# Expert results added to the output: the order of two waits, a third result buffer, and weights converted in halves

## The chip, the cores and the metric

The kernel runs on one core of a Trainium2 chip. The metric is the device time of one execution in microseconds (us), the median over the timed runs. Beside it there is one execution with the hardware profiler, whose time and trace are used for every duration below. In it PE is TensorE's matmul row, DVE is VectorE, ACT is ScalarE, POOL is GpSimd and SP is SyncE.

## The reference

The input `x` has 8 x 256 = 2048 tokens of 256 numbers. A gated cross-attention picks two of 64 sets for each token and adds their weighted mean; then a gated mixture of experts follows, in which each token goes to 2 of 8 experts. The second part takes most of the time:

```python
x = x + jnp.tanh(g_xattn[0]) * _L0_xattn_ref(_layernorm(x), ctx_2048, ...)
x = x + jnp.tanh(g_ffn[0]) * _L0_ffn_ref(_layernorm(x), ...)
# in _L0_ffn_ref, for each of 8 experts (256 -> 1024 -> 256), w the token's weight for it:
h = jax.nn.gelu(xf @ w1 + b1, approximate=False)
y = h @ w2 + b2
acc = acc + y * w[:, None]
```

## The kernel before

**First stage** (to about 80 us). Tokens are loaded, attention and routing are computed, and `x` after attention is written to `out` in device memory. The normalised rows go to `xrows`. A table is made that sorts the 4096 pairs of token and expert by expert into 36 tiles of 128 rows. 32 tiles belong to one expert each; four, tiles 25, 28, 31 and 34 (`mixed_of`, `MIXED_AT`, `MIXED_STEP`), hold 64 rows of one expert and 64 of another.

**Weights.** There are 16 units (`NU`), fc1 and fc2 of each expert, each 128 x 2048 in fp32 in its own region of `wreg`. A unit is converted into two fp16 parts, the high part by ACT (`weights_hi`, L934) and the remainder by DVE (`weights_lo`, L1566), which waits for ACT by the semaphore `w_hi` and reports by `w_lo`. The parts go to the region that the unit ahead has left, so ACT's next unit waits for `w_lo`. Units 0 and 1 are done ahead of tile 0 in halves of 1024 columns (`first_hi`, `first_lo`, L925 and L1559). `units_of_tile` (L394) names the tile in whose place each other unit stands: unit 2 at tile 1, 3 at 3, then 4 to 15 at tiles 4, 6, 8, 10, 12, 14, 16, 17, 19, 20, 22, 23. `unit_ready` is PE's wait for a unit.

**A tile** i passes through these steps, each in the order of its engine's own program; semaphores alone tie the engines together.

- POOL fetches its 128 rows by an indirect DMA (`fetch_rows`, L1843), five tiles ahead; SP transposes them by a DMA.
- PE multiplies by the fc1 weights in 8 chunks of 128 columns, 6 matmuls each (L704). Between these chunks stand the chunks of fc2 for earlier tiles, 3 matmuls each (L730): the second half of tile i-2, then the first half of tile i-1. A mixed tile's fc2 comes all at once after the next tile's fc1.
- ACT applies GELU in two halves (L1018); DVE splits each half into two fp16 parts (`split`, L1736 and L1738), for which fc2 waits.
- DVE scales fc2's result and adds the bias (`add_bias`, L1695) into one of two buffers `y_sb`; ACT multiplies by the token's weight (`weigh`, L1057) in place and reports by `y_ready`.
- POOL adds the 128 rows to `out` by an indirect DMA with accumulation (`add_tile`, L1864; a mixed tile's halves in two transfers, L1856 and L1860). A token appears in two tiles, so each transfer waits by the semaphore `added` until the one ahead has landed. `add_bias` waits for the add two tiles back, whose buffer it fills.

For a mixed tile DVE copies the second expert's weights into buffers of their own ahead of time: `keep_w1` (four copies, L1715) two tiles ahead, `keep_w2` (L1727) one tile ahead; fc1 of the mixed tile waits for the first. `keep_w1` of tile 25 also waits until all units are converted.

A wait written right ahead of an instruction isn't always an instruction of its own. Of several waits in a row the built program puts one into the instruction itself, the last of the list in the rows of order below; the others become wait instructions ahead of it.

Of the kernel before, what the change touches and what calls it, by code (L numbers as in the profile page):

```python
# [5 lines left out]
ALU = mybir.AluOpType  # L6
ACT = mybir.ActivationFunctionType
AX = mybir.AxisListType
# [25 lines left out]
def flamingo_block(nc, x, ctx_sets, token_sets, g_xattn, g_ffn, desc, w_q, b_q, gate_w, gate_b,  # L34
# [42 lines left out]
    with ExitStack() as stack:  # L77
# [162 lines left out]
        by_half = table_buf[:, 2 * TILES * E:2 * TILES * E + 3 * E * E].rearrange("p (k s e) -> p k s e", k=3, e=E)  # L240
        half = sb("half", [P, 3, E])
        is_odd = sb("is_odd", [P, 2, MIXED], F16)
# [19 lines left out]
        def at_mixed(row):  # L262
# [129 lines left out]
        NARROW, WIDE = 160, 36  # L392
        units_of_tile = {1: (2,), 3: (3,)}
# [75 lines left out]
        def _(pe):  # L469
# [185 lines left out]
            def unit_ready(k):  # L655

                if k < 2:
                    pe.wait_ge(half_lo, 2 * k + 2)
                else:
                    pe.wait_ge(w_lo, k - 1)  # L660

# [21 lines left out]
            def fc1(i, c, ws):  # L683

                part_f = c // (FC // 2)
                if c == 0:
                    if i < FIRST_BY_PE:
                        pe.wait_ge(x0_sb, i + 1)
                    else:
                        pe.wait_ge(xT_in[i % NX], transposed(i))  # L690
                    if i == 0 or unit_for(i) != unit_for(i - 1):
                        unit_ready(unit_for(i))
                if c % (FC // 2) == 0 and i >= 2:
                    pe.wait_ge(gelu_done, 2 * (i - 2) + part_f + 1)
                if c == 0 and i in mixed_of:
                    pe.wait_ge(w1_kept, mixed_of[i] + 1)
                rows_each = P // len(ws)
                for h, of_half in enumerate(ws):
                    at = c % (FC // 2) * P + h * rows_each
                    put = bank[2 * (i % 2) + part_f][:, at:at + rows_each]  # L700
                    for k in range(KC):
                        hi, lo = of_half[k]
                        for n, (w, x_part) in enumerate(((hi, 0), (hi, 1), (lo, 0))):
                            mm = pe.matmul(put, w, xT[:, i % NX, x_part, k, h * rows_each:(h + 1) * rows_each],  # L704
                                           start=(k == 0 and n == 0), stop=(k == KC - 1 and n == 2))
                if c % (FC // 2) == FC // 2 - 1:
                    mm.then_inc(fc1_ps, 1)
# [111 lines left out]
        def _(act):  # L819
# [108 lines left out]

            def weights_hi(k, at):
                if k == 2:  # L930
                    act.wait_ge(half_lo, 4)
                else:
                    act.wait_ge(w_lo, k - 2)
                act.activation(whalf[:, bass.ds(at[1], 1), 0:UNIT].rearrange("p a n -> p (a n)"),  # L934
                               wreg[:, bass.ds(at[0], 1), :].rearrange("p a n -> p (a n)"),
                               ACT.Copy, scale=W_SCALE).then_inc(w_hi, 1)

            copy_pair(0, 0)
# [116 lines left out]
            def weigh(i):  # L1055
                act.wait_ge(y_biased, i + 1)
                act.activation(y_sb[:, i % 2, :], y_sb[:, i % 2, :], ACT.Copy,  # L1057
                               scale=wcur[:, i % NX:i % NX + 1]).then_inc(y_ready, 1)

            for i in range(TILES):  # L1060
                if i == TILES - 1:
                    weigh(i - 2)
                gelu(i, 0)
                if i == 0:
                    copy_rows(1)
                if 2 <= i < TILES - 1:
                    weigh(i - 2)
                if i + 1 < TILES:
                    fetch(i + 1)
                gelu(i, 1)  # L1070
                for k in units_of_tile.get(i, ()):
                    weights_hi(k, unit_regions(k))
            for i in range(TILES - 2, TILES):
# [3 lines left out]
        def _(v):  # L1077
# [381 lines left out]
            def odd_halves(k):  # L1459
# [35 lines left out]
                if k == 9:  # L1495
                    v.tensor_reduce(half[:, :, :], by_half, AX.X, ALU.add).then_inc(vec_step, 1)
                    done.up()
                if k == 10:
                    v.scalar_tensor_tensor(out=is_pair[:, :], in0=at_mixed(per_tile[:, 1, :]), scalar=0.0, in1=at_mixed(is_col),
                                           op0=ALU.is_gt, op1=ALU.mult).then_inc(halves_ready, 1)  # L1500
                    v.tensor_scalar(is_odd[:, :, :], half[:, 1, :].rearrange("p (m h) -> p h m", h=2), -1.0, iota_p[:, 0:1],
                                    ALU.add, ALU.is_equal).then_inc(halves_ready, 1)
                    v.tensor_tensor(code_m[:, :].rearrange("a (m h) -> a m h", h=2),
                                    half[0:1, 2, :].rearrange("a (m h) -> a m h", h=2),
                                    at_mixed(per_tile[0:1, 2, :]).unsqueeze(2).to_broadcast([1, MIXED, 2]),
                                    ALU.add).then_inc(vec_step, 1)
                    v.tensor_scalar(real_m[:, :, :], half[0:H, 0, :].rearrange("p (m h) -> p h m", h=2), iota_p[0:H, 0:1], None,
                                    ALU.is_gt).then_inc(vec_step, 1)
# [54 lines left out]

            def weights_lo(k, at):
                v.wait_ge(w_hi, k - 1)
                v.scalar_tensor_tensor(out=whalf[:, bass.ds(at[1], 1), UNIT:2 * UNIT].rearrange("p a n -> p (a n)"),  # L1566
                                       in0=wreg[:, bass.ds(at[0], 1), :].rearrange("p a n -> p (a n)"), scalar=W_SCALE,
                                       in1=whalf[:, bass.ds(at[1], 1), 0:UNIT].rearrange("p a n -> p (a n)"),
                                       op0=ALU.mult, op1=ALU.subtract).then_inc(w_lo, 1)

            pick_sets(0)
# [114 lines left out]
            def add_bias(i):  # L1686
# [3 lines left out]
                if i == 0:  # L1690
                    v.wait_ge(b2_in, 16)
                if i >= 2:
                    v.wait_ge(added, added_by(i - 2))
                for at, e in experts[i]:
                    op = v.scalar_tensor_tensor(out=y_sb[at, i % 2, :], in0=bank[ypos[i % 2]][at, 0:D],  # L1695
                                                scalar=1.0 / (H_SCALE * W_SCALE),
                                                in1=b2_all[at, bass.ds(e, 1), :].rearrange("p a d -> p (a d)"),
                                                op0=ALU.mult, op1=ALU.add)
# [4 lines left out]
            def keep_w1(m):  # L1703
                if m == 0:
                    v.wait_ge(w_lo, NU - 2)
                    v.wait_ge(out_init, 16 * NG)
# [12 lines left out]
            def keep_w2(m):  # L1719
                if m == 0:  # L1720
                    v.wait_ge(w_lo, NU - 2)
                if m >= 1:
# [21 lines left out]
            for i in range(TILES):  # L1744
# [8 lines left out]

                for k in units_of_tile.get(i - 1, ()):
                    if k < 4:
                        weights_lo(k, unit_regions(k))
                split(i, 1)
# [6 lines left out]
                if i == 18:  # L1764
                    odd_halves(13)
                for k in units_of_tile.get(i, ()):
                    if k >= 4:
                        weights_lo(k, unit_regions(k))
                if i + 2 in mixed_of:
# [7 lines left out]
        def _(pool):  # L1777
# [69 lines left out]
            def add_tile(i):  # L1847
                pool.wait_ge(y_ready, i + 1)
                if i >= 1:
                    pool.wait_ge(added, added_by(i - 1))  # L1850
                if i in mixed_of:

                    if i == MIXED_AT:
# [3 lines left out]
                        out=out[:, :], out_offset=bass.IndirectOffsetOnAxis(ap=add_m[:, 0, m:m + 1], axis=0),  # L1857
                        in_=y_sb[0:H, i % 2, :], in_offset=None, compute_op=ALU.add).then_inc(added, 16)
                    pool.wait_ge(added, added_by(i) - 16)
                    pool.indirect_dma_start(  # L1860
                        out=out[:, :], out_offset=bass.IndirectOffsetOnAxis(ap=add_m[:, 1, m:m + 1], axis=0),
                        in_=y_sb[H:P, i % 2, :], in_offset=None, compute_op=ALU.add).then_inc(added, 16)
                    return
                pool.indirect_dma_start(  # L1864
                    out=out[:, :], out_offset=bass.IndirectOffsetOnAxis(ap=add_at[:, i:i + 1], axis=0),
                    in_=y_sb[:, i % 2, :], in_offset=None, compute_op=ALU.add).then_inc(added, 16)

# [40 lines left out]
```

## Time and profile before

| | |
|---|---|
| median of the runs | 307.14 us (306.23, 307.14, 511.84) |
| profiled execution | 307.81 us |
| its span in the trace | 306.0 us |
| PE busy | 249.3 us (81% of the span) |
| DVE, ACT, POOL busy | 214.6, 182.9, 145.0 us |

The span is the time from the first to the last recorded event; the profiled execution's time is 1.8 us longer than its span, and 0.67 above the median. Busy shares are averages over stages with different limits, so the stages are read one by one. An idle time in a row belongs to the instruction behind it: "[0.84 <-DVE rows L1738]" says that the engine stood 0.84 us ahead of this instruction, and that DVE's instruction of line 1738 ended it.

### The profile page before, as it was taken

Reading aid. Unit: us, or ns where it says so; the run is one execution under the profiler, and the core shown is the slowest. Engines: PE = TensorE matmul, PEld = TensorE weight load, DVE = VectorE, ACT = ScalarE, POOL = GpSimd, SP = SyncE. Lnnn points to the kernel's source line nnn. Section 1 sums busy time; section 2 is a strip of 40 time slices with the busy share of each in tenths; the row PEclk is TensorE's granted clock in tenths of the full one; section 3 lists DMA queues with packets and bytes.
Section 4 is the critical chain, followed back from the end, with each engine's and each line's share of the span. In section 5 each row is a group of like instructions: output and inputs, shape, how many; then the busy total and the mean of one; then the engine's idle time right before and its main releaser. Section 6 shows DMA issues by size and latency. Waiting matters only on the chain.

```text
span 306.0 us, 9678 instructions
## 1 busy us (share of the span) xinstructions
PE 249.3 (81%) x3353; PEld 232.6 (76%) x3353; DVE 214.6 (70%) x679; ACT 182.9 (60%) x579; POOL 145.0 (47%) x122
## 2 busy tenths in 40 slices
PE   1999919734799999999999999998699999997100
PEld 1999818634699989999999999987698999996100
DVE  3898799997988778677777777767767666763100
ACT  1143869696684776866686776686474856573100
POOL 2121128994524657577454454366353635523330
PEclk9996955855899999999999999999799999999855
DMA  6999999986314434564635435346344342432220
GB/s 179 341 372 376 380 372 378 375 305 208 93 39 88 71 54 71 84 86 64 106 64 78 82 62 90 55 59 99 45 69 75 50 88 36 73 44 28 22 21 10
DMA packets 44575, 39.75 MB, mean 130 GB/s; under 512 B 21361, under 2 KB 41202, under 8 KB 44402
## 3 DMA queue, kind: packets, MB, share of 16 engines
q1 hardware_dynamic: 36912, 29.22, 31.3%
q0 software_dynamic: 6976, 9.59, 21.3%
q8 instruction: 29, 0.48, 0.7%
q10 hardware_dynamic: 642, 0.33, 0.4%
q14 instruction: 16, 0.13, 0.1%
HBM read 25.70 MB, written 8.98 MB: 113 GB/s over the span
## 4 chain that ended last, share of the span: by engine, by line
PE 40%; DMA 16%; DVE 14%; issue 9%; ACT 4%; POOL 2%; DVEq 1%; POOLq 0%; ACTq 0%
PE bank L704 21%; PE bank L730 18%; DMA out_dram<-xn,add_at 9%; DMA out_dram<-xn,add_m 6%; ACT wreg L934 2%; DVE wreg L1566 2%; ACT rows L1018 1%; DVE wreg L1237 1%; DVE rows L1228 1%; DVE xs L1207 1%; DMA xs<-xrows,fetch_at 1%; POOL out_dram L1856 1%; DVE earlier L1281 1%; DVE gmark L1271 1%; POOL out_dram L1864 1%
## 5 line engine op out<-in xcount | busy, mean ns | idle before, releaser
L730 PE MATMUL bank<-wreg,rows 128*128 (+1 forms) x864 | 135.8, 274 | 3.1 <-DVE rows L1738 3.1
L704 PE MATMUL bank<-xTp,wreg 128*128 128x128 f16 (+1 forms) x1728 | 132.5, 217 | 5.7 <-DVE pick_buf L1715 3.4
L704 PEld LDWEIGHTS bank<-xTp,wreg 128*128 x1728 | 113.1, 98 | 14.4 <-issue 7.0
L1018 ACT ACTIVATE rows<-bank,maskbias 128x128 f32<-128x128 f32 (+1 forms) x320 | 86.4, 363 | 24.2 <-issue 19.7
L1864 POOL DMA_INDIRECT out_dram<-xn,add_at x32 | 55.2, 1724 | 69.7 <-ACT maskbias L1049 34.3
L730 PEld LDWEIGHTS bank<-wreg,rows 128*128 128x128 f16 (+1 forms) x864 | 74.3, 99 | 7.3 <-issue 3.6
L1736 DVE TENSOR_SCALAR rows<-rows 128x512 f16<-128x512 f32 x72 | 31.9, 443 | 36.5 <-ACT rows L1018 36.2
L1738 DVE SCALAR_TENSOR_TENSOR rows<-rows 128x512 f16<-128x512 f32 x72 | 49.9, 693 | 2.5
L1843 POOL DMA_INDIRECT xs<-xrows,fetch_at x32 | 40.4, 1262 | 20.8 <-issue 9.1
L1057 ACT ACTIVATE xn<-xn,maskbias 128x256 f32<-128x256 f32 x36 | 18.5, 514 | 44.9 <-DVE xn L1695 44.9
L1566 DVE SCALAR_TENSOR_TENSOR wreg<-wreg x14 | 32.1, 2292 | 10.6 <-ACT wreg L934 9.7
L934 ACT ACTIVATE wreg<-wreg x14 | 26.9, 1919 | 2.1 <-DVE wreg L1566 1.9
L1804 POOL TENSOR_TENSOR rs<-ve,neg_half 128x4 f32<-128x4 f32 x8 | 8.4, 1050 | 34.6 <-DVE ve L1089 20.6
L1695 DVE SCALAR_TENSOR_TENSOR xn<-bank,xs 128x256 f32<-128x256 f32 (+1 forms) x40 | 16.8, 420 | 8.6 <-DMA out_dram<-xn,add_at 4.0
L830 ACT ACTIVATE xTp<-bank 128x512 f32<-128x512 f32 x8 | 4.8, 597 | 13.9 <-PE bank L477 13.9
L1856 POOL DMA_INDIRECT out_dram<-xn,add_m x4 | 6.1, 1534 | 13.9 <-DMA out_dram<-xn,add_at 7.4
L477 PE MATMUL bank<-ident,xs 128*128 128x128 f32 x32 | 7.2, 383 | 6.3 <-DMA xs<-in_x_dram 6.3
L1812 POOL TENSOR_SCALAR at_col<-iota,place_f,token 128x128 f16<-128x128 f32 x12 | 12.0, 1008 | 0.0
L490 PE MATMUL bank<-rhs_c,xTp 128*128 128x73 f32 x64 | 11.4, 336 | 0.0
L730 PE MATMUL bank<-xn,rows 128*64 128x256 f16 x80 | 11.2, 274 | 0.0
L490 PEld LDWEIGHTS bank<-rhs_c,xTp 128*128 128x128 f32 x64 | 10.7, 253 | 0.1
L477 PEld LDWEIGHTS bank<-ident,xs 128*128 128x128 f32 x32 | 6.0, 213 | 6.3 <-issue 6.3
(270 smaller groups left out, 338.2 us busy)
## 6 DMA issues: line engine op xcount, KB each, us to landing
wreg<-in_L_ffn_fc_w_dram SPq DMA_DIRECT2D x16, 1024.0 KB, 13.0
xrows<-rows SPq DMA_DIRECT2D x4, 528.0 KB, 5.9
xs<-in_x_dram SPq DMA_DIRECT2D x4, 512.0 KB, 8.8
out_dram<-xs SPq DMA_DIRECT2D x4, 512.0 KB, 8.6
xs<-in_L_ffn_fc_b_dram SPq DMA_DIRECT2D x1, 1024.0 KB, 5.9
xTp<-xs SPq DMA_TRANSPOSE x34
ctx_sb<-in_ctx_dram SPq DMA_DIRECT2D x1, 512.0 KB, 8.8
xs<-xrows,fetch_at POOLq DMA_INDIRECT x32
```

The source lines that it names most:

```text
L490: mm = pe.matmul(bank[2 + g % 2][:, q * NR:(q + 1) * NR], xTp[:, j, t, k, :], rhs_c[:, k, :], start=(k == 0), stop=(k == KC - 1))
L704: mm = pe.matmul(put, w, xT[:, i % NX, x_part, k, h * rows_each:(h + 1) * rows_each], start=(k == 0 and n == 0), stop=(k == KC - 1 and n = ...
L730: mm = pe.matmul(yb[at, :], h_part[:, at], of_half[w_part], start=(c == 0 and n == 0), stop=(c == FC - 1 and n == 2))
L934: act.activation(whalf[:, bass.ds(at[1], 1), 0:UNIT].rearrange("p a n -> p (a n)"), wreg[:, bass.ds(at[0], 1), :].rearrange("p a n -> p (a ...
L1018: op = act.activation(h32[i % 2][:, f * P:(f + 1) * P][:, at], bank[2 * (i % 2) + half][:, c * P:(c + 1) * P][:, at], ACT.Gelu, bias=bias[ ...
L1057: act.activation(y_sb[:, i % 2, :], y_sb[:, i % 2, :], ACT.Copy, scale=wcur[:, i % NX:i % NX + 1]).then_inc(y_ready, 1)
L1566: v.scalar_tensor_tensor(out=whalf[:, bass.ds(at[1], 1), UNIT:2 * UNIT].rearrange("p a n -> p (a n)"), in0=wreg[:, bass.ds(at[0], 1), :].r ...
L1695: op = v.scalar_tensor_tensor(out=y_sb[at, i % 2, :], in0=bank[ypos[i % 2]][at, 0:D], scalar=1.0 / (H_SCALE * W_SCALE), in1=b2_all[at, bas ...
L1736: v.tensor_scalar(hhi[i % 2][:, c], h32[i % 2][:, c], H_SCALE, None, ALU.mult).then_inc(hi_done, 1)
L1738: v.scalar_tensor_tensor(out=hlo[i % 2][:, c], in0=h32[i % 2][:, c], scalar=H_SCALE, in1=hhi[i % 2][:, c], op0=ALU.mult, op1=ALU.subtract) ...
L1843: pool.indirect_dma_start(out=xg[:, i % NXG, :], out_offset=None, in_=xrows[:, :], in_offset=bass.IndirectOffsetOnAxis(ap=rows_at, axis=0) ...
L1864: pool.indirect_dma_start(out=out[:, :], out_offset=bass.IndirectOffsetOnAxis(ap=add_at[:, i:i + 1], axis=0), in_=y_sb[:, i % 2, :], in_of ...
```

## The change

Four things change. The waits in `add_tile` change places, so that the wait for the add ahead is now the one inside the transfer. `y_sb` has three buffers (`NY`), the third in the place of `wT`, which the first stage has finished with; `add_bias` waits for the add three tiles back. Units 2 to 15 are converted in halves of 1024 columns on ACT and DVE, each half counted by `w_hi` and `w_lo`, and the halves of units 4 to 15 are spread over tiles 4 to 22 (a table gives the tile of the first half and of the second). PE's wait for units at tile 25 asks for the last unit. A tensor is renamed (`half` to `of_half_slot`), which moves nothing.

```diff
-        y_sb = xn[:, 0, 0:2, :]
+        y_sb = [xn[:, 0, 0, :], xn[:, 0, 1, :], wT[:, :, :].rearrange("n u p -> n (u p)")]
+        NY = len(y_sb)
...
-        for k, i in zip(range(4, NU), (4, 6, 8, 10, 12, 14, 16, 17, 19, 20, 22, 23)):
-            units_of_tile[i] = (k,)
+        units_of_tile = {1: ((2, 0), (2, 1)), 3: ((3, 0), (3, 1))}
+        for k, (i, j) in zip(range(4, NU), ((4, 5), (6, 7), (8, 8), (9, 10), (11, 11), (12, 13), (14, 15), (16, 16), (17, 18),
+                                            (19, 19), (20, 21), (22, 22))):
+            units_of_tile[i] = units_of_tile.get(i, ()) + ((k, 0),)
+            units_of_tile[j] = units_of_tile.get(j, ()) + ((k, 1),)
...
-                    if i == 0 or unit_for(i) != unit_for(i - 1):
+                    if i == MIXED_AT:
+                        unit_ready(NU - 1)
+                    elif i == 0 or unit_for(i) != unit_for(i - 1):
                         unit_ready(unit_for(i))
...
+            def weights_hi(k, half):
+
+                if half == 0:
+                    unit_at[0] = unit_regions(k)
+                    if k == 2:
+                        act.wait_ge(half_lo, 4)
+                    else:
+                        act.wait_ge(w_lo, 2 * (k - 2))
+                at = unit_at[0]
+                c = slice(half * (UNIT // 2), (half + 1) * (UNIT // 2))
+                act.activation(whalf[:, bass.ds(at[1], 1), c].rearrange("p a n -> p (a n)"),
+                               wreg[:, bass.ds(at[0], 1), c].rearrange("p a n -> p (a n)"),
                                ACT.Copy, scale=W_SCALE).then_inc(w_hi, 1)
...
+            def weights_lo(k, half):
+
+                if half == 0:
+                    unit_at[0] = unit_regions(k)
+                at = unit_at[0]
+                v.wait_ge(w_hi, 2 * (k - 2) + half + 1)
...
-                if i >= 2:
-                    v.wait_ge(added, added_by(i - 2))
+                if i >= NY:
+                    v.wait_ge(added, added_by(i - NY))
...
             def add_tile(i):
-                pool.wait_ge(y_ready, i + 1)
                 if i >= 1:
                     pool.wait_ge(added, added_by(i - 1))
+                pool.wait_ge(y_ready, i + 1)
```

On POOL, from the fetch ahead of the first add of tile 25 to the add of tile 26, this stood in a row before (the waits in brackets in the order in which they are met, the last one inside the instruction):

```order
L1843 DMA xs<-xrows,fetch_at 128x264 [waits cur_ready,xT_in2]
L1856 DMA out_dram<-xn,add_m 2176x256 [waits add_m_ready,added,y_ready]
L1860 DMA out_dram<-xn,add_m 2176x256 [waits added]
L1843 DMA xs<-xrows,fetch_m 128x264 [waits cur_ready,xT_in3]
L1864 DMA out_dram<-xn,add_at 2176x256 [waits added,y_ready]
```

and this stands there now:

```order
L1861 DMA xs<-xrows,fetch_at 128x264 [waits cur_ready,xT_in2]
L1874 DMA out_dram<-xn,add_m 2176x256 [waits add_m_ready,y_ready,added]
L1878 DMA out_dram<-xn,add_m 2176x256 [waits added]
L1861 DMA xs<-xrows,fetch_m 128x264 [waits cur_ready,xT_in3]
L1882 DMA out_dram<-wT,add_at 2176x256 [waits y_ready,added]
```

No instruction moved; in L1856 and L1864 the semaphore inside the transfer was `y_ready` and is `added`, as it always was in L1860.

On DVE, from the second split of tile 23 to the copies of `keep_w1` for tile 25, this stood before (`w_hi` is ACT's report of unit 15):

```order
L1736 TENSOR_SCALAR rows<-rows 128x512 [waits y_ps,gelu_done]
L1738 SCALAR_TENSOR_TENSOR rows<-rows 128x512 [waits hi_done]
L1566 ISA [waits w_hi]
L1566 ISA
L1566 SCALAR_TENSOR_TENSOR wreg<-wreg 128x2048
L1709 TENSOR_LOAD tw_m [waits out_init,w_lo]
L1715 ISA
L1715 COPY xs<-wreg 128x1024
```

and this stands there now:

```order
L1754 TENSOR_SCALAR rows<-rows 128x512 [waits y_ps,gelu_done]
L1756 SCALAR_TENSOR_TENSOR rows<-rows 128x512 [waits hi_done]
L1729 TENSOR_LOAD tw_m [waits out_init,w_lo]
L1735 ISA
L1735 COPY xs<-wreg 128x1024
```

Unit 15 moved from there to one tile earlier, where unit 14 had been; unit 14's halves are at tiles 20 and 21.

On ACT, behind the GELU of tile 22's second half, this stood before:

```order
L1018 ACTIVATE rows<-bank,maskbias 128x128 x3
L915 TENSOR_LOAD units_i
L934 ISA [waits w_lo]
L934 ACTIVATE wreg<-wreg 128x2048
L1018 ACTIVATE rows<-bank,maskbias 128x128 [waits lo_done,fc1_ps,cur_ready]
```

and this stands there now:

```order
L1030 ACTIVATE rows<-bank,maskbias 128x128 x3
L944 ISA [waits w_lo]
L944 ACTIVATE wreg<-wreg 128x1024
L944 ISA
L944 ACTIVATE wreg<-wreg 128x1024
L1030 ACTIVATE rows<-bank,maskbias 128x128 [waits lo_done,fc1_ps,cur_ready]
```

One instruction of 2048 columns became two of 1024, and only the first of them waits.

## Rows read from the trace of the kernel before

**Rows 1.** The page's second part: busy tenths of PE in 40 slices.

```profile
PE   1999919734799999999999999998699999997100
```

**Rows 2.** The chain of waits from 228 us on: start, us, what.

```profile
241.50 4.04 DMA out_dram<-xn,add_at
246.29 6.43 DMA out_dram<-xn,add_at
...
274.77 0.27 issue
275.04 3.18 DMA out_dram<-xn,add_m
...
278.25 0.71 issue
...
295.56 1.56 POOL out_dram L1864
```

**Rows 3.** POOL's timeline: start, us, instruction, count, idle time before and releaser.

```profile
217.70 1.71 POOL L1864 DMA_INDIRECT out_dram<-xn,add_at  x1 [5.62 <-ACT xn L1057]
...
234.25 1.46 POOL L1856 DMA_INDIRECT out_dram<-xn,add_m  x1 [3.20 <-ACT xn L1057]
237.63 1.42 POOL L1860 DMA_INDIRECT out_dram<-xn,add_m  x1 [1.93 <-DMA out_dram<-xn,add_m]
239.36 1.10 POOL L1843 DMA_INDIRECT xs<-xrows,fetch_m  x1 [0.31 <-issue]
...
246.29 1.98 POOL L1864 DMA_INDIRECT out_dram<-xn,add_at  x1 [1.85 <-DMA out_dram<-xn,add_at]
```

**Rows 4.** ACT's timeline, same columns: results weighted, tiles 23, 25, 27, 28.

```profile
216.92 0.51 ACT L1057 ACTIVATE xn<-xn,maskbias 128x256 f32<-128x256 f32 x1 [4.05 <-DVE xn L1695]
...
232.81 0.52 ACT L1057 ACTIVATE xn<-xn,maskbias 128x256 f32<-128x256 f32 x1
...
243.74 0.52 ACT L1057 ACTIVATE xn<-xn,maskbias 128x256 f32<-128x256 f32 x1
...
249.60 0.52 ACT L1057 ACTIVATE xn<-xn,maskbias 128x256 f32<-128x256 f32 x1
```

**Rows 5.** PE's timeline: four gaps, and the row before the longest.

```profile
113.01 0.49 PE L730 MATMUL bank<-wreg,rows 128*128 x3 [0.36 <-DVE rows L1738]
...
199.64 0.49 PE L730 MATMUL bank<-wreg,rows 128*128 x3 [0.84 <-DVE rows L1738]
...
212.80 0.49 PE L730 MATMUL bank<-wreg,rows 128*128 x3
216.70 0.48 PE L704 MATMUL bank<-xTp,wreg 128*128 128x64 f16 x6 [3.41 <-DVE pick_buf L1715]
...
281.76 2.78 PE L730 MATMUL bank<-wreg,rows 128*128 x24 [1.91 <-DVE rows L1738]
```

**Rows 6.** PE by stretch: from:to, us, busy (instructions), granted clock, DMA share, GB/s.

```profile
216.70:219.20 2.50, 2.50 (x30) 0.50 0.13 27
```

**Rows 7.** DVE's timeline, same columns as rows 3.

```profile
210.53 0.69 DVE L1738 SCALAR_TENSOR_TENSOR rows<-rows 128x512 f16<-128x512 f32 x1
212.12 2.29 DVE L1566 SCALAR_TENSOR_TENSOR wreg<-wreg  x1 [0.89 <-ACT wreg L934]
215.12 0.43 DVE L1715 COPY xs<-wreg 128x1024 f16 x1 [0.71 <-DVE wreg L1566]
...
216.13 0.42 DVE L1715 COPY pick_buf<-wreg 128x1024 f16 x1
...
246.67 0.43 DVE L1715 COPY xs<-wreg 128x1024 f16 x1
...
278.43 0.42 DVE L1695 SCALAR_TENSOR_TENSOR xn<-bank,xs 128x256 f32<-128x256 f32 x1 [2.66 <-DMA out_dram<-xn,add_m]
```

**Rows 8.** Line 1559, halves of units: duration in ns min/median/max, first and last start.

```profile
L1559 DVE SCALAR_TENSOR_TENSOR wreg<-wreg x4: 1226/1226/1247, 76.5 to 81.9; 128x1024 f16<-128x1024 f16 x2, - x2
```

**Rows 9.** The page's fifth part: the high part of a split.

```profile
L1736 DVE TENSOR_SCALAR rows<-rows 128x512 f16<-128x512 f32 x72 | 31.9, 443 | 36.5 <-ACT rows L1018 36.2
```

More of the change, by code:

```diff
@@ L240, in flamingo_block @@
         by_half = table_buf[:, 2 * TILES * E:2 * TILES * E + 3 * E * E].rearrange("p (k s e) -> p k s e", k=3, e=E)
-        half = sb("half", [P, 3, E])
+        of_half_slot = sb("of_half_slot", [P, 3, E])
         is_odd = sb("is_odd", [P, 2, MIXED], F16)
@@ L1056, in weigh @@
                 act.wait_ge(y_biased, i + 1)
-                act.activation(y_sb[:, i % 2, :], y_sb[:, i % 2, :], ACT.Copy,
+                act.activation(y_sb[i % NY], y_sb[i % NY], ACT.Copy,
                                scale=wcur[:, i % NX:i % NX + 1]).then_inc(y_ready, 1)
@@ L1070, in _ @@
                 gelu(i, 1)
-                for k in units_of_tile.get(i, ()):
-                    weights_hi(k, unit_regions(k))
+                for k, half in units_of_tile.get(i, ()):
+                    weights_hi(k, half)
             for i in range(TILES - 2, TILES):
@@ L1495, in odd_halves @@
                 if k == 9:
-                    v.tensor_reduce(half[:, :, :], by_half, AX.X, ALU.add).then_inc(vec_step, 1)
+                    v.tensor_reduce(of_half_slot[:, :, :], by_half, AX.X, ALU.add).then_inc(vec_step, 1)
                     done.up()
@@ L1562, in first_lo @@
                                        op0=ALU.mult, op1=ALU.subtract).then_inc(half_lo, 1)
[L1564 to L1568, printed above, removed]
+            def weights_lo(k, half):
[3 more added lines that the diff above has]
+                v.wait_ge(w_hi, 2 * (k - 2) + half + 1)
+                c = slice(half * (UNIT // 2), (half + 1) * (UNIT // 2))
+                low = slice(UNIT + half * (UNIT // 2), UNIT + (half + 1) * (UNIT // 2))
+                v.scalar_tensor_tensor(out=whalf[:, bass.ds(at[1], 1), low].rearrange("p a n -> p (a n)"),
+                                       in0=wreg[:, bass.ds(at[0], 1), c].rearrange("p a n -> p (a n)"), scalar=W_SCALE,
+                                       in1=whalf[:, bass.ds(at[1], 1), c].rearrange("p a n -> p (a n)"),
                                        op0=ALU.mult, op1=ALU.subtract).then_inc(w_lo, 1)
+            unit_at = [None]
             pick_sets(0)
@@ L1752, in _ @@
                     table_rest()
-                for k in units_of_tile.get(i - 1, ()):
+                for k, half in units_of_tile.get(i - 1, ()):
                     if k < 4:
-                        weights_lo(k, unit_regions(k))
+                        weights_lo(k, half)
                 split(i, 1)
@@ L1765, in _ @@
                     odd_halves(13)
-                for k in units_of_tile.get(i, ()):
+                for k, half in units_of_tile.get(i, ()):
                     if k >= 4:
-                        weights_lo(k, unit_regions(k))
+                        weights_lo(k, half)
                 if i + 2 in mixed_of:
@@ L1861, in add_tile @@
                         out=out[:, :], out_offset=bass.IndirectOffsetOnAxis(ap=add_m[:, 1, m:m + 1], axis=0),
[L1862 removed]
+                        in_=y_sb[i % NY][H:P, :], in_offset=None, compute_op=ALU.add).then_inc(added, 16)
                     return
@@ L1865, in add_tile @@
                     out=out[:, :], out_offset=bass.IndirectOffsetOnAxis(ap=add_at[:, i:i + 1], axis=0),
-                    in_=y_sb[:, i % 2, :], in_offset=None, compute_op=ALU.add).then_inc(added, 16)
+                    in_=y_sb[i % NY], in_offset=None, compute_op=ALU.add).then_inc(added, 16)
             pool.wait_ge(out_init, 16 * NG)
```

25 lines of the change are left out of this document (8 added, 17 removed).

## The prediction

> **What bounds the kernel now.** I read the page first. Its row of PE in 40 slices [rows 1] is at 9 tenths from the twelfth slice to the thirty-sixth but for one dip to 8 and 6, and nearly empty in the last three: for some 20 us at the end something else sets the time. The chain of waits over the last 78 us names it [rows 2]: a chain of the adds alone, transfer after transfer, from the first add of tile 25 (234.25) [rows 3] to that of tile 35 (295.56). PE has ended its last matmul at 281.76 + 2.78 = 284.54 [rows 5], 11 us before the last add starts. So two limits follow each other: up to the result of tile 25 PE does (its gaps are those of rows 5, and each moves everything behind it), and from there on the adds, each of which may start only when the one ahead has landed.
>
> In the chain there are 15 transfers (tiles 25, 28, 31, 34 have two), so 14 links. Four links are those from a mixed tile's first half to its second (L1860); there the wait for the add ahead already stands in the transfer itself. After the landing of the transfer at 271.47 the second half starts 0.27 us later (275.04) [rows 2]. The other ten links have that wait as an instruction of its own ahead of the transfer: the one at 275.04 lands at 278.22 and after 0.71 us of "issue", from 278.25 on, the next starts at 278.96, 0.74 later [rows 2].
>
> **The order of the waits.** Ten links change from the second form to the first: 10 x (0.74 - 0.27) = 4.7 us. L1860 has no fetch between itself and the add ahead, the ten have one; the nearest row for that is the add of tile 23, which had a fetch ahead and its result's wait inside: ACT ends at 216.92 + 0.51 = 217.43 and the add starts at 217.70, again 0.27 later [rows 3, 4]. So I take 0.47 for each; the bounds are 0 (nothing saved) and 0.74 (all saved), that is 0 to 7.4 us. What leaves the inside, the wait for the result y, is passed early: y of tile 27 was ready at 243.74 + 0.52 = 244.26 and its add started at 246.29; of tile 28, 250.12 against 253.47 [rows 3, 4], which is 0.75 after the transfer of 27 landed (246.29 + 6.43 = 252.72) [rows 2]. With 0.74 between y and a start, tile 27 leaves 1.29 us, and the two links up to there save 0.94: the chain stays bound by landings. Where y comes last the new order costs the same 0.47, which falls on adds ahead of tile 25 that nobody waits for, and once, at most, on the first add of tile 25 (at 234.25 already 0.92 behind its result of 232.81 + 0.52 [rows 3, 4], so I count nothing). Behind an add on POOL stand only the fetch and the next add; the fetch fits into the flight: 1.42 + 0.31 + 1.10 = 2.83 us of POOL [rows 3], where such a transfer takes 3.18 [rows 2].
>
> The trace shows that the descriptors are not written ahead of the landing: POOL's 1.42 us of L1860 begin at 237.63, after its wait of 1.93 us [rows 3]. The Trainium skill, "DMA: Bandwidth & Descriptors", section "Anatomy of one DMA", has it so too: DMA engines do not wait on semaphores, the issuing sequencer does so before dispatch. By it the wait "inside" hides no descriptor writing, and the sum stays at 0.47 a link.
>
> **The conversion in halves, done by tile 22.** The largest gap of PE is 3.41 us before tile 25, until DVE's copies of weights for the first mixed tile are done [rows 5]. On DVE they stand behind the low half of unit 15 (212.12, 2.29 us), which waited for ACT [rows 7]. Now that unit is at tile 22, and after the split that ends at 210.53 + 0.69 = 211.22 only the copies follow: 0.71 for the load of the region's number (215.12 less 214.41), 1.43 for the four (215.12 to 216.55), so 213.36, and PE 0.15 later, 213.51. PE was free at 212.80 + 0.49 = 213.29 [rows 5, 7]. Gain 3.2 us; at worst none, if the halves end late, at best 3.41.
>
> After that gap PE ran at half speed: granted clock 0.50, the 1.2 GHz level, from 216.70 to 219.20, all 2.50 us busy [rows 6]. At full speed the same matmuls take 1.25. After the gap of 0.84 at 199.64 three matmuls took the same 0.49 as those at 212.80 [rows 5], so a short gap doesn't do that, and without the long one 1.25 us come back.
>
> Two more gaps, 0.36 at 113.01 and 0.84 at 199.64, wait for a split on DVE [rows 5] that stood behind a whole unit. A half takes 1.23 us on DVE against 2.29 for a whole [rows 7, 8], and the first half's can run while ACT does the second. I count both gaps as gone, 1.2 us (bounds 0 and 1.2). The 14 units cost 14 x (2 x 1.23 - 2.29) = 2.4 us more on DVE, all beside PE: DVE's work in a tile is then about 2 x (0.43 + 0.69) + 0.42 + 1.23 = 3.9 us, or 5.1 where both halves fall together, and results come 5.9 us apart (tile 27 to 28) [rows 4, 7 to 9].
>
> **The third buffer.** DVE waited 2.66 us for the landing of the first add two tiles back at 278.43, and PE had 1.91 us of idle time behind it at 281.76 [rows 5, 7]. With three buffers that goes and PE ends 1.9 us sooner; but the chain of adds ends last, and in it each y was there already. Worth 0 at the end.
>
> **The sum.** PE reaches tile 25's result 3.2 + 1.25 + 1.2 = 5.65 us sooner, and all of the chain starts with it; the chain is 4.7 shorter: 10.35 us. The profiled execution took 307.81 (span 306.0), so 297.5; the median 307.14 is 0.67 below it, so I forecast **296.8**, 3.4% faster. Its own spread: the transfer of tile 27 took 6.43 us where that of 26 took 4.04 [rows 2]; without such a one the chain is held by y of tile 28 instead, at most 1.2 better (250.12 + 0.74 against 253.47 less 1.41), and one more of it costs 2.4. With both short gaps kept it is 298.0. Its own range is 294.5 to 299.5.
>
> DVE copies beside an add can make it longer: the add at 246.29 kept POOL for 1.98 us, with copies from 246.67 on, that at 217.70 for 1.71 [rows 3, 7]. The Trainium skill, "SBUF — State Buffer", section "Who interferes with whom", says that copies in a two-port mode lock GpSimd out for the whole instruction. Five groups of copies still come after the first add of tile 25; by that rule, if all five fell on an add and each cost the 0.27 us between these rows, the sum would be 298.1, within the forecast's own range, and I give it one chance in ten.
>
> **Rivals.** (1) *The link saves nothing*, since the time is POOL's start after any wait: 307.14 - 5.65 = 301.5. Against it: two rows with 0.27, of two kinds of transfer. Chance 0.09. (2) *Tile 25 still waits*, because ACT or DVE end unit 15 late: only the chain's 4.7 and perhaps 1.2 remain, 301.2 to 302.4. For it: in my sum the copies already end 0.2 us after PE is free. Chance 0.09. (3) *Slower: conversions now touch every tile.* From tile 4 to tile 22 all 19 tiles have a half or two behind their splits, where 12 had a unit. If each holds PE for the 0.84 us seen at 199.64, that is 16.0, less 1.2 that were there, less 4.45 and 4.7: +5.6, 312.8; it decides from the point where DVE's 3.9 us and its waits for ACT pass the tile's time. Against it: 2 of 12 whole units left a gap. Slower by any amount needs 0.55 a tile. Chance 0.05. (4) *The wait inside lets POOL write descriptors ahead*: then the chain falls behind PE, and the last add starts near 279 (PE's end 284.54 less 1.91 and 5.65, then 0.42 for the bias, 0.51 for the weight and 0.74) instead of 295.56: 291; row L1860 speaks against it. Chance 0.04. (5) *The change doesn't do what it says*, the built program's waits being reordered: their order on POOL is as shown above, so this is within (1). The rest, 0.73, is the forecast.
>
> **How the numbers follow.** The range 294 to 302 holds the forecast's spread and (1) and most of (2); outside are (3), (4) and a part of the tails, below 0.2. Two per cent, about what a measurement of this kernel can tell from no change, lie at 301.0 and 313.3. Faster than that: the forecast and (4), and small parts of (1) and (2), 0.79; within: most of (1) and (2), half of (3), some tail, 0.18; slower: 0.03.
>
> **What would show it.** The chain of waits after: again adds from tile 25 on, with about 0.27 between landing and next start in all 14 links (right), or 0.7 (rival 1). PE: no gap before its first 128x64 matmuls and no half clock behind it; no gap near 113 and 199; if gaps of 0.5 or more stand at many tiles up to 22, rival 3. DVE's bias without a wait for an add at the end, PE's last gap gone. The forecast is wrong if transfers take longer once they follow more closely, as their length is taken from before.

## The result, and the profile after

The changed kernel takes 293.4 us, the median of four runs, against 307.4 of the kernel before in the same comparison: ratio 0.9555, 95% interval 0.9514 to 0.9597. In a later comparison, with six runs against eleven, it was 293.44 against 305.28, ratio 0.9634 (0.9595 to 0.9672). A few executions took far longer than the rest (511.84 us for the kernel before); the ratios leave them out. The forecast was 296.8 with a range of 294 to 302: the sign and the kinds of gain were right, the size was too small by 3.4 us, and the result lies 0.6 below the range.

The profiled execution of it took 292.61 us, its span 290.8, which is 15.2 less than before. The page's second part first, PE and the clock that it was granted, in 40 slices:

```profile
PE   1999718733899999999999999999999999999500
...
PEclk9999955855799999999999999999999999999965
```

The dip to 8 and 6 in the twenty-eighth and twenty-ninth slices [rows 1] is gone. PE's timeline around tile 25 (start, us, instruction, count; a wait would stand in brackets), and its last row:

```profile
208.31 0.49 PE L735 MATMUL bank<-wreg,rows 128*128 x3
208.64 0.34 PE L709 MATMUL bank<-xTp,wreg 128*128 128x64 f16 x6
...
270.34 2.79 PE L735 MATMUL bank<-wreg,rows 128*128 x24
```

The 3.41 us ahead of tile 25, the two short waits and the one of 1.91 at the end [rows 5] are gone. The window behind the start of tile 25 (columns as in rows 6) is at full clock, where it was 0.50:

```profile
208.64:211.14 2.50, 2.50 (x61) 1.00 0.34 56
```

On DVE the copies for tile 25 follow the split directly, and the last ends at 207.76, 0.9 us before PE asks for them:

```profile
205.29 0.69 DVE L1756 SCALAR_TENSOR_TENSOR rows<-rows 128x512 f16<-128x512 f32 x1
206.30 0.43 DVE L1735 COPY xs<-wreg 128x1024 f16 x1 [0.32 <-issue]
...
207.35 0.41 DVE L1735 COPY pick_buf<-wreg 128x1024 f16 x1
```

The chain of waits still ends in adds (start, us, what):

```profile
236.51 4.54 DMA out_dram<-xn,add_at
241.05 0.52 issue
241.57 1.65 POOL out_dram L1874
...
249.32 4.71 DMA out_dram<-wT,add_at
254.03 0.27 issue
254.29 3.82 DMA out_dram<-xn,add_at
258.11 0.27 issue
258.38 3.55 DMA out_dram<-xn,add_m
261.93 0.27 issue
262.19 3.04 DMA out_dram<-xn,add_m
...
280.13 0.27 issue
280.39 1.56 POOL out_dram L1882
```

From 254 on the 0.27 us that stood only ahead of a mixed tile's second half [rows 2] stands in each link. The 0.52 ahead of 241.57 is not set by the landing: 0.27 behind it would have been 241.32. The result of tile 28 came late there. ACT ended it at 240.28 + 0.52 = 240.80, and the add started 0.77 behind it, as it did 0.76 behind it in e10:

```profile
240.28 0.52 ACT L1069 ACTIVATE xn<-xn,maskbias 128x256 f32<-128x256 f32 x1
```

The last add starts 15.2 us sooner than before, and 10.4 us from there to the span's end are as they were. The 15.2 can be divided by three marks, the starts of tile 0's first fc1, tile 25's first fc1 and tile 25's first add:

| stage | before | after | difference |
|---|---|---|---|
| to tile 0's first fc1 | 80.40 | 78.14 | 2.26 |
| from there to tile 25's | 136.30 | 130.50 | 5.80 |
| to tile 25's first add | 17.55 | 16.17 | 1.38 |
| chain of adds, to tile 35's | 61.31 | 55.58 | 5.73 |

The first stage's 2.26 us were in nobody's sum, since nothing is changed there. The experiments had to say which of these differences belong to the change, which part of it brings each, and why the second is larger than forecast.

### The profile page after: what moved, and what is told of

It is laid out like the page before. It is cut to its first block, busy times and chain, and to the rows that moved or that the text cites. A ratio compares the mean times of both kernels' runs of the same rounds, so it can differ in the third digit from the quotient of the medians.

```text
span 290.8 us, 9747 instructions
## 1 busy us (share of the span) xinstructions
PE 244.2 (84%) x3353; PEld 228.6 (79%) x3353; DVE 215.4 (74%) x693; ACT 183.8 (63%) x593; POOL 146.8 (50%) x122
## 4 chain that ended last, share of the span: by engine, by line
PE 53%; DMA 12%; issue 4%; DVE 3%; POOL 2%; ACT 1%; DVEq 0%; POOLq 0%; ACTq 0%
PE bank L709 27%; PE bank L735 25%; DMA out_dram<-xn,add_at 4%; DMA out_dram<-xn,add_m 3%; DMA out_dram<-wT,add_at 3%; DMA xs<-xrows,fetch_at 1%; POOL out_dram L1874 1%; ACT rows L1030 1%; POOL out_dram L1882 1%; DVE rows L1240 1%; DVE wreg L1249 0%; POOL out_dram L1878 0%; POOL xs L1861 0%; ACT xTp L1011 0%; PE bank L629 0%
## 5 line engine op out<-in xcount | busy, mean ns | idle before, releaser
L1861 POOL DMA_INDIRECT xs<-xrows,fetch_at x32 | 43.4, 1357 | 20.8 <-issue 9.1
L1882 POOL DMA_INDIRECT out_dram<-xn,add_at x20 | 32.3, 1616 | 41.3 <-ACT maskbias L1061 33.6
L1756 DVE SCALAR_TENSOR_TENSOR rows<-rows 128x512 f16<-128x512 f32 x72 | 49.8, 692 | 2.5
L1584 DVE SCALAR_TENSOR_TENSOR wreg<-wreg x28 | 33.6, 1220 | 3.7 <-issue 1.6
L944 ACT ACTIVATE wreg<-wreg x28 | 29.0, 1064 | 2.0 <-DVE wreg L1584 2.0
L1882 POOL DMA_INDIRECT out_dram<-wT,add_at x12 | 20.7, 1726 | 17.9 <-ACT maskbias L1061 11.5
L1069 ACT ACTIVATE xn<-xn,maskbias 128x256 f32<-128x256 f32 x24 | 12.3, 511 | 21.5 <-DVE xn L1715 21.5
L1715 DVE SCALAR_TENSOR_TENSOR xn<-bank,xs 128x256 f32<-128x256 f32 (+1 forms) x28 | 11.7, 419 | 0.9 <-PE bank L735 0.3
L1069 ACT ACTIVATE wT<-wT,maskbias 128x256 f32<-128x256 f32 x12 | 6.3, 523 | 8.5 <-DVE wT L1715 8.5
L480 PE MATMUL bank<-ident,xs 128*128 128x128 f32 x32 | 6.3, 347 | 5.9 <-DMA xs<-in_x_dram 5.9
L493 PE MATMUL bank<-rhs_c,xTp 128*128 128x73 f32 x64 | 10.5, 318 | 0.1
```

Of the source, the lines that this page charges most:

```text
L944: act.activation(whalf[:, bass.ds(at[1], 1), c].rearrange("p a n -> p (a n)"), wreg[:, bass.ds(at[0], 1), c].rearrange("p a n -> p (a n)") ...
L1069: act.activation(y_sb[i % NY], y_sb[i % NY], ACT.Copy, scale=wcur[:, i % NX:i % NX + 1]).then_inc(y_ready, 1)
L1584: v.scalar_tensor_tensor(out=whalf[:, bass.ds(at[1], 1), low].rearrange("p a n -> p (a n)"), in0=wreg[:, bass.ds(at[0], 1), c].rearrange(" ...
L1715: op = v.scalar_tensor_tensor(out=y_sb[i % NY][at, :], in0=bank[ypos[i % 2]][at, 0:D], scalar=1.0 / (H_SCALE * W_SCALE), in1=b2_all[at, ba ...
L1756: v.scalar_tensor_tensor(out=hlo[i % 2][:, c], in0=h32[i % 2][:, c], scalar=H_SCALE, in1=hhi[i % 2][:, c], op0=ALU.mult, op1=ALU.subtract) ...
L1861: pool.indirect_dma_start(out=xg[:, i % NXG, :], out_offset=None, in_=xrows[:, :], in_offset=bass.IndirectOffsetOnAxis(ap=rows_at, axis=0) ...
```

## The experiments

Each comparison is with runs of the kernel before on the same chip, whose medians were 305.78 (e1 to e4), 306.29 (e5 to e8) and 305.28 us (e9 to e12).

**e1, the order of the waits alone.** In the kernel before:

```diff
             def add_tile(i):
-                pool.wait_ge(y_ready, i + 1)
                 if i >= 1:
                     pool.wait_ge(added, added_by(i - 1))
+                pool.wait_ge(y_ready, i + 1)
```

> The kernel before, and only the two waits of the add change places. Theory (each of ten links of the chain of adds is 0.47 us shorter): 307.1 less 4.7 is 302.4, with 0.27 between a landing and the next start in all links of the trace. Rival (the wait's place is worth nothing, the time between the two kernels comes from the halves): 307.1, with 0.7 in the ten links. If the 2.3 us by which the first stage was shorter in the changed kernel are the chance of one execution, they may show up here too, though nothing of the first stage is changed; if they belong to the halves, tile 0's first fc1 starts near 80.4 as before.

Measured: 301.48 us, ratio 0.9857 (0.9788 to 0.9925). Its chain of waits:

```profile
270.29 0.27 issue
270.55 3.15 DMA out_dram<-xn,add_m
273.70 0.27 issue
273.96 4.15 DMA out_dram<-xn,add_at
278.11 0.27 issue
278.38 4.00 DMA out_dram<-xn,add_at
```

The links behind a landing are 0.27, also the one from 273.70, which had been 0.74 before (278.22 to 278.96) [rows 2]. The theory holds, and the rival, that the place is worth nothing, falls: the interval leaves out 1, though it is wide, 2.3 to 6.5 us. Tile 25 still waited 3.82 us on PE, so results came later than in the changed kernel, and two links, ahead of tiles 28 and 31, waited for a result (1.81 and 1.53 us from landing to start).

**e2, the halves by tile 22 alone:** the changed kernel with two buffers and the old order of the waits.

```diff
-        y_sb = [xn[:, 0, 0, :], xn[:, 0, 1, :], wT[:, :, :].rearrange("n u p -> n (u p)")]
+        y_sb = [xn[:, 0, 0, :], xn[:, 0, 1, :]]
...
             def add_tile(i):
+                pool.wait_ge(y_ready, i + 1)
                 if i >= 1:
                     pool.wait_ge(added, added_by(i - 1))
-                pool.wait_ge(y_ready, i + 1)
```

> The kernel before, and only the conversion in halves by tile 22 (old order of the waits, two buffers). Theory (all waits of PE up to tile 25 go, the short ones that the timeline does not list too, and the half clock behind the longest): 7.0 us from PE, the chain of adds as long as before, so 300.1. The forecast's own size, 5.65 us, gives 301.5. Rival (the first stage's 2.3 us belong to the halves): 297.8, with tile 0's first fc1 near 78.1. Rival (the tail is as long as its adds whatever PE does): 307.

Measured: 297.12 us, ratio 0.9687 (0.9608 to 0.9765), or 7.2 to 12.0 us less than 305.78. That is more than the forecast's own 5.65, and the interval lies just above the theory's 7.0. The time is near the rival's 297.8, but not for its reason: tile 0 began at 78.89, later than in e3, which has no halves. No wait of PE for DVE up to tile 25 is left, and from tile 0 to tile 25 it took 130.13 us.

**e3, the third buffer alone,** in the kernel before (`y_sb` and `NY` as in the change).

> The kernel before, and only the third result buffer. Theory (worth 0 at the end, since each result on the chain was there before its add could start): 307.1, with PE's last gap of 1.91 us gone and the last add starting as late as before. Rival (a result two tiles back holds the chain somewhere): 305.2 or less, by the 1.91 us of PE's gap.

Measured: 306.0 us, ratio 1.0033 (0.9993 to 1.0073). PE's last 24 matmuls start without a wait, and the end doesn't move. Its tile 0 began at 77.98, though no instruction ahead of it differs from the kernel before: the 2.3 us of the first stage don't belong to the halves.

**e4, the changed kernel without the third buffer.**

> The changed kernel without its third buffer. Theory (worth nothing here too): 293.4, the links still 0.27. Rival (with the shorter chain results come just in time, and a bias that waits for the add two tiles back makes the result late for its own add): 294.4 to 295.3, and the chain of waits goes through DVE's bias and ACT's weight in its last third.

Measured: 293.66 us, ratio 0.9601 (0.9541 to 0.9662), the same as with it. DVE waits again for an add near the end,

```profile
274.33 0.42 DVE L1715 SCALAR_TENSOR_TENSOR xn<-bank,xs 128x256 f32<-128x256 f32 x1 [2.22 <-DMA out_dram<-xn,add_at]
```

and the last add, at 281.36, starts 7 us behind this bias. The buffer is worth 0 in either kernel.

**e5, whole units by tile 22,** in the kernel before:

```diff
-        for k, i in zip(range(4, NU), (4, 6, 8, 10, 12, 14, 16, 17, 19, 20, 22, 23)):
+        for k, i in zip(range(4, NU), (4, 6, 8, 10, 12, 14, 16, 17, 19, 20, 21, 22)):
```

> The kernel before, its units still converted whole, but the last four at tiles 19, 20, 21 and 22 instead of 19, 20, 22 and 23; nothing else is changed. Theory (the earlier end alone takes PE's longest wait, 3.6 us over its normal pace, and the half clock behind it, 1.25; the short waits at splits stay): 4.8 us less than before, 301 if before is 305.8 as in the runs ahead of this, and the first matmuls of tile 25 without a wait. Rival (whole units at four tiles in a row make PE wait at each, 0.8 to 1.0 as at 199.64): 302 to 304, with three or four waits of PE on splits between 185 and 210 us.

Measured: 304.98 us, ratio 0.9994 (0.9952 to 1.0035): no gain that the runs can tell, 1.5 us at most, and longer than theory and rival had it. PE's timeline has what the rival said:

```profile
197.64 0.49 PE L730 MATMUL bank<-wreg,rows 128*128 x3 [0.89 <-DVE rows L1738]
204.10 0.49 PE L730 MATMUL bank<-wreg,rows 128*128 x3 [0.82 <-DVE rows L1738]
...
210.56 0.49 PE L730 MATMUL bank<-wreg,rows 128*128 x3 [0.45 <-DVE rows L1738]
214.02 0.34 PE L704 MATMUL bank<-xTp,wreg 128*128 128x64 f16 x6 [0.88 <-DVE pick_buf L1715]
```

The wait ahead of tile 25 fell from 3.4 to 0.88, but waits at splits took its place, and PE reached tile 25 only 0.6 us sooner (135.67 behind tile 0's start, against 136.3). PE kept its clock behind that wait (columns as in rows 6):

```profile
214.02:215.22 1.20, 1.20 (x29) 1.00 0.35 106
```

So the first add of tile 25 started 152.1 us behind tile 0's first fc1, 1.9 sooner than in the mean of before, e9, e1 and e3. The chain of adds, with the old order, then took 62.51, the longest among the traces whose mixed tiles stand at 25, 28, 31 and 34, and in this execution used that up. The earlier end alone pays little, then, and much less than the halves in e2.

**e6 and e7, the changed kernel with both halves of a unit at one tile,** the last at 22 (e6) or at 23 (e7, which has the table of the kernel before):

```diff
-        for k, (i, j) in zip(range(4, NU), ((4, 5), (6, 7), (8, 8), (9, 10), (11, 11), (12, 13), (14, 15), (16, 16), (17, 18),
-                                            (19, 19), (20, 21), (22, 22))):
-            units_of_tile[i] = units_of_tile.get(i, ()) + ((k, 0),)
-            units_of_tile[j] = units_of_tile.get(j, ()) + ((k, 1),)
+        for k, i in zip(range(4, NU), (4, 6, 8, 10, 12, 14, 16, 17, 19, 20, 21, 22)):
+            units_of_tile[i] = ((k, 0), (k, 1))
```

> The changed kernel, but both halves of a unit always at one tile: units 4 to 15 at tiles 4, 6, 8, 10, 12, 14, 16, 17, 19, 20, 21, 22. Theory (a half on ACT lets DVE start 1 us sooner, which is what takes the short waits): 293.4, no waits of PE. Rival (it is the spreading over two tiles that takes them): up to 1.5 us more, 294.9, with PE's short waits at splits back near 111 and 196 us.

> The changed kernel, but each unit's two halves stand at the tile where the whole unit stood, the last at 23. Theory (the early end is what takes the long wait): PE waits before tile 25 again for DVE's copies, about 1 us less than the 3.4 of before since DVE's first half runs beside ACT's second, so 2.5 us, and 1.25 for the half clock if so long a wait still brings it: 296 to 297. Rival (halving alone takes the wait, the place is free): 293.4.

Measured: e6 298.22 us, ratio 0.975 (0.9663 to 0.9837); e7 297.96, ratio 0.973 (0.9635 to 0.9826). Both are slower than any expectation for them. No wait at a split is listed in either, which for e6 speaks against its rival; but tile 25 waits, in e6

```profile
212.22 0.34 PE L707 MATMUL bank<-xTp,wreg 128*128 128x64 f16 x6 [1.16 <-DVE pick_buf L1733]
```

and in e7, where 2.5 had been expected:

```profile
211.42 0.34 PE L707 MATMUL bank<-xTp,wreg 128*128 128x64 f16 x6 [1.84 <-DVE pick_buf L1733]
```

The clock stayed up behind both waits, in e6 and in e7:

```profile
212.22:213.42 1.20, 1.20 (x29) 1.00 0.46 119
```

```profile
211.42:212.42 1.00, 1.00 (x27) 1.00 0.47 90
```

So PE's wait ahead of tile 25 is 3.4 us with whole units up to 23, 1.84 with halves up to 23, 0.88 with whole units up to 22, 1.16 with pairs of halves at 19 to 22, and none in the changed kernel's table, where tiles 20 and 21 have one half each. Halving takes the short waits; it needs the spreading as well to take the long one. Both kernels are 4.5 to 4.8 us slower than the changed one (293.44). The stages of their traces explain 3.0 of it in e6 and 3.9 in e7, against the means of the last table below; the rest lies within the intervals and stays open.

**e8, the mixed tiles at 25, 27, 29 and 31** in the changed kernel (`MIXED_STEP` 2).

> The changed kernel with its four mixed tiles at 25, 27, 29 and 31 instead of 25, 28, 31 and 34, so that the last four tiles have one transfer each. Theory (the adds bind from tile 27 to the end, a pure tile's add of 4 us gives back 1 to 1.5 us against PE's 5.3 a tile, and tile 34's second transfer of 3.3 us leaves the end, where results come fast): the last add starts 1.8 us sooner, 291.6. Rival (the chain of adds is bound all the way, so that the order of its transfers cannot matter): 293.4. Rival (mixed tiles nearer to each other make DVE's copies or the second expert's weights late): 295 or more, with PE waits before tiles 27, 29 or 31.

Measured: 293.05 us, ratio 0.9589 (0.9493 to 0.9686), not to be told from the changed kernel. POOL's timeline, the last four adds:

```profile
268.85 1.56 POOL L1882 DMA_INDIRECT out_dram<-wT,add_at  x1 [2.51 <-DMA out_dram<-xn,add_m]
272.93 1.56 POOL L1882 DMA_INDIRECT out_dram<-xn,add_at  x1 [2.51 <-ACT xn L1069]
276.99 1.55 POOL L1882 DMA_INDIRECT out_dram<-xn,add_at  x1 [2.51 <-DMA out_dram<-xn,add_at]
281.04 1.55 POOL L1882 DMA_INDIRECT out_dram<-wT,add_at  x1 [2.49 <-DMA out_dram<-xn,add_at]
```

They follow each other at the pace of transfers, 4.05 to 4.08 us, though ACT had the result of tile 35 ready at 274.85. The row at 272.93 names ACT, but the result that came there is tile 34's; its own, tile 33's, had long been ready:

```profile
266.90 0.51 ACT L1069 ACTIVATE xn<-xn,maskbias 128x256 f32<-128x256 f32 x1 [1.55 <-DVE xn L1715]
```

The theory of 1.8 us falls: counted from tile 25's first fc1, the first add of tile 25 came 1.3 us later than in the changed kernel, and the chain was 1.35 shorter.

**e11 and e12, the mixed tiles earlier still,** every second tile from 24 and from 23, with halves packed more closely (the edit of e11; that of e12 has 23 and a closer table):

```diff
-    MIXED_AT, MIXED_STEP, MIXED = 25, 3, E // 2
+    MIXED_AT, MIXED_STEP, MIXED = 24, 2, E // 2
...
+        for k, (i, j) in zip(range(4, NU), ((4, 5), (6, 6), (7, 8), (9, 9), (10, 11), (12, 12), (13, 14), (15, 15), (16, 17),
+                                            (18, 18), (19, 20), (21, 21))):
```

> The changed kernel with its mixed tiles at 24, 26, 28 and 30, and the halves done by tile 21 (two of them at tiles 6, 9, 12, 15, 18 and 21). Theory (the adds bind from about tile 29 on; from there to the last add are then eight transfers where there were nine, so one of 3.3 us leaves the end, and results allow 275): last add near 277, 290.5. Rival (denser conversions make PE wait again, as whole units did at tiles 20 to 22): 294 or more, with waits of PE on splits or before tile 24. Rival (the adds bind from tile 24 on, so that their order does not matter): 293.4.

> The same with mixed tiles at 23, 25, 27 and 29 and the halves done by tile 20 (two of them at tiles 5, 8, 11, 14, 17, 19 and 20). Theory: two transfers of 3.3 us fewer behind tile 29 than in the changed kernel, so that the last add waits for its result and not for a landing: 275.2, 288.5. Rival (conversions are too dense): 294 or more, PE waits. Rival (the adds bind all the way): 293.4.

Measured: e11 293.92 us, ratio 0.9616 (0.9566 to 0.9667); e12 300.42, ratio 0.9841 (0.9803 to 0.988). Theory missed in both. In e11 the last add started at 283.29 with its result ready at 276.18: the adds bind all the way. In e12 they do too, but the rival of dense conversions came true as well. PE's waits at splits are back, the first and the longest of six:

```profile
118.95 0.49 PE L735 MATMUL bank<-wreg,rows 128*128 x3 [0.65 <-DVE rows L1756]
...
187.03 0.49 PE L735 MATMUL bank<-wreg,rows 128*128 x3 [1.15 <-DVE rows L1756]
```

PE reached tile 23 there 128.42 us behind tile 0's first fc1, later than it reached tile 24 in e11 (125.46); a part of that is a stretch at half clock, from 80.1 to 83.5, that e11 doesn't have. No version beat the changed kernel.

**e9 and e10, both kernels again, unchanged.**

> The kernel before, unchanged, for its trace. Theory (tile 0's first fc1 at 80.40 was the chance of one execution: in eight other traces it stands at 78.0 to 80.0, with the same first stage): 78 to 80, PE's waits up to tile 25 the same 6 to 7 us over its pace, the chain of adds from tile 25's first to tile 35's 60 to 62.5 us. Rival (the first stage of this kernel is always 2 us longer): 80.4 again.

> The changed kernel, unchanged. Theory (PE's waits and half clock 7.4 us, ten links 4.6, the rest of the first difference is chance): 306 less 12.0, 294.0, ratio 0.961, tile 0's first fc1 anywhere from 78 to 80, the chain 55.5 to 57 us. Rival (the whole difference of the two first traces belongs to the change): 15.2 less than 306, 290.8.

Measured: e9 303.05 us (one execution), tile 0's first fc1 at 78.10, not 80.40; e10 293.44, ratio 0.9634. The chain of adds took 58.38 in e9, less than the 60 to 62.5 expected. The first stage's 2.26 us were the chance of one execution: in the thirteen other traces tile 0 starts from 77.98 to 79.96. With the second execution of the kernel before, the same marks over all traces say what each part is worth:

| stage | without the part | with it | worth |
|---|---|---|---|
| tile 0 to tile 25 on PE | 136.30, 135.84, 135.92, 137.10 (before, e9, e1, e3) | 130.50, 130.67, 130.13, 130.28 (after, e10, e2, e4) | 5.9 |
| tile 25 to its first add | 17.55, 18.46, 17.44, 17.50 (same) | 16.17, 16.17, 15.73, 16.17 (same) | 1.7 |
| chain of adds | 61.31, 58.38, 59.92, 60.32, 62.51 (before, e9, e3, e2, e5) | 55.58, 55.55, 56.71, 56.08, 57.04, 56.85 (after, e10, e1, e4, e6, e7) | 4.2 |

The differences of the means add up to 11.8 us; the medians of the last comparison differ by 305.28 - 293.44 = 11.84.

## Why the prediction was right in kind and too small in size

**The chain of adds** was right. Ten links of 0.47 were to give 4.7 us; the traces' means give 4.2, and e1 alone gives 4.3 in the medians (305.78 - 301.48). Added up from landing to start, the ten links take 7.8 to 7.9 us in all five traces of the old order, 2.7 to 3.3 in five of the new, and 5.5 in e1, where two wait for results. The 14 transfers between them are no shorter: 49.4 to 53.6 us with the old order, 50.2 to 53.1 with the new. Their spread is chance, for the chain of one and the same kernel took 61.31 and 58.38 in two executions, so the 5.73 between the first two traces holds over a microsecond of it. Rival 1 is out, and rival 5 with it.

**The conversion in halves** is the step that failed, "3.2 + 1.25 + 1.2 = 5.65 us sooner": a mis-sized term, which measured 5.9 + 1.7 = 7.6. The working behind it read PE's waits off the rows as they stand in brackets. In e9, the kernel before again:

```profile
109.42 0.49 PE L730 MATMUL bank<-wreg,rows 128*128 x3
109.75 0.50 PE L704 MATMUL bank<-xTp,wreg 128*128 128x128 f16 x6
110.54 0.49 PE L730 MATMUL bank<-wreg,rows 128*128 x3 [0.29 <-DVE rows L1738]
...
195.56 0.50 PE L704 MATMUL bank<-xTp,wreg 128*128 128x128 f16 x6
196.89 0.49 PE L730 MATMUL bank<-wreg,rows 128*128 x3 [0.84 <-DVE rows L1738]
```

These rows start 0.33 us apart while each is 0.5 long, since matmuls overlap. A row that starts 0.79 behind the last has lost 0.46, not 0.29; one that starts 1.33 behind has lost 1.00, not 0.84. The bracket counts from the modelled end of the row ahead and leaves out 0.17 every time. Counted by starts, the kernel before lost 2.0 us up to tile 24 in three places (0.53, 1.01, and 0.48 at 207.83, which the bracket gives as 0.32 of issue and the forecast left out, below), and 3.57 ahead of tile 25, together 5.6; waits under 0.25 make the rest of the 5.9. The forecast had 1.2 and 3.2, and for the short ones it even gave 1.2 as the upper bound.

```profile
207.02 0.49 PE L730 MATMUL bank<-wreg,rows 128*128 x3
207.83 0.49 PE L704 MATMUL bank<-xTp,wreg 128*128 128x128 f16 x6 [0.32 <-issue]
```

**The half clock** was counted at 1.25 us from one execution; the stage behind it shrank by 1.7 on average (in e5, e6 and e7, whose clock stayed up, it took 16.42, 16.47 and 16.89, so not all of the 1.7 need be the clock's). How long the clock stays down differs: 0.50 for 2.5 us and a little more before [rows 6], but in e9, behind a wait of the same 3.4 us:

```profile
213.94:214.94 1.00, 1.00 (x14) 0.50 0.00 0
...
217.94:218.94 1.00, 1.00 (x15) 0.50 0.52 96
218.94:219.94 1.00, 1.00 (x20) 0.76 0.59 85
```

some 5.5 us at half speed, which cost 2.7. By the clock's fall and rise in the four traces with the long wait, half speed cost 1.3 (before), 1.4 (e1), 1.7 (e3) and 2.7 (e9), 1.8 on average.

**The base** was the third miss. The forecast starts from 307.81, a profiled execution whose first stage was the slowest of fourteen traces, and ends at a median of three runs; eleven to thirteen runs gave 305.3 to 306.3. Against 307.14 that is 0.9 to 1.9 us, and 1.4 (11.8 - 10.35) was missed in the terms: together 2.3 to 3.3 of the 3.4. Between the two first traces the forecast missed by 297.5 - 292.61 = 4.9: 2.3 of the first stage, 1.5 of the halves (5.80 + 1.38 against 5.65) and 1.0 of the chain (5.73 against 4.7), which held the transfer of 6.43 [rows 2] that the forecast had named as worth up to 1.2.

**The third buffer** was worth 0, as forecast, in both kernels (e3, e4). **Rival 2** (tile 25 still waits) is what e6 and e7 did with 1.16 and 1.84 us, so the forecast's 0.2 us of margin was a fair warning; in the changed kernel the copies end 0.9 us early. **Rival 3** (conversions hold PE at many tiles) didn't happen here, but its mechanism is real: the waits at splits are there in e5 and e12. **Rival 4** is out: with the wait inside the transfer POOL's own row still begins 0.27 behind the landing.

The rule from the Trainium skill, "SBUF — State Buffer", section "Who interferes with whom", that copies in a two-port mode lock GpSimd out, was given one chance in ten to cost 1.35 us. In the trace after, POOL's rows of adds don't follow the copies: the add with none beside it is the long one, the add whose start falls among four copies of L1735 is short.

```profile
249.32 2.20 POOL L1882 DMA_INDIRECT out_dram<-wT,add_at  x1 [1.20 <-DMA out_dram<-xn,add_m]
254.29 1.60 POOL L1882 DMA_INDIRECT out_dram<-xn,add_at  x1 [1.25 <-DMA out_dram<-wT,add_at]
```

```profile
254.01 0.43 DVE L1735 COPY xs<-wreg 128x1024 f16 x1
...
255.02 0.60 DVE L1735 COPY pick_buf<-wreg 128x1024 f16 x1
```

DVE was not idle beside the long one (L1756 from 249.20, L1715 from 250.24), so these rows speak of the copies alone. What makes some transfers last 4.7 to 6.4 us instead of 3.8 to 4.0 wasn't tried.

## What to carry to other kernels

In a chain of dependent transfers, put the wait that comes last inside the transfer: here that was worth 4.2 us over ten links, and the order of two lines decided it. Where an engine's instructions overlap, count a wait from the pace of starts, not from the end of the row ahead, and search for lost pace below the smallest wait that a view lists. And work that is moved into the cover of other work pays only if it is cut small enough to fit at each place: here whole units ended earlier (e5) brought nothing that the runs could tell, halves in pairs (e6) part of the gain, spread halves all of it.

## What the runs showed of the hardware that was not expected

PE's clock fell to half behind waits of 3.4 and 3.8 us (before, e1, e3, e9) and not behind 0.88, 1.16 and 1.84 (e5, e6, e7); once down, PE worked at half speed for 2.7 us (before, e1), 3.4 (e3) and 5.5 (e9), busy all along, until the clock rose. In a chain of indirect adds without fetches between them one follows the other in 4.0 to 4.2 us for 128 rows (265.50 to 269.47 to 273.70 in the trace after, and the end of e8), and mostly in 3.3 to 3.4 for 64 rows (262.19 to 265.50 in the trace after; 3.8 from 258.38). So half the rows cost some four fifths of the time: the four tiles with two transfers are dear, and moving them about didn't help (e8, e11), since every transfer waits for the one ahead.
